# Routing logits of a mixture-of-experts block computed transposed, in four column strips of the TensorE array

## The chip, the cores and the metric

One NeuronCore of a Trainium2 chip. The metric is the device time of one execution in microseconds (us). Before the change the median of three runs is 702.88 us (702.61 to 703.27).

## What is computed

The input x is 8 sequences of 1024 tokens with 128 features, all in fp32. The kernel applies three layers, each with a residual: a feed-forward layer with half weight, a causal attention with one head, and the same feed-forward layer again.

```python
x = x + 0.5 * ffn(layernorm(x))
x = x + attention(layernorm(x))
x = x + 0.5 * ffn(layernorm(x))

# ffn(flat), T tokens, H = 128, E = 16 experts of width 64, and one shared expert of width 128
scores = sigmoid(flat @ Wg.T)                      # routing logits: T x 16
topk_idx, topk_w = route(scores, bias_corr)        # best 2 of 4 groups, then the best 4 experts
cw = zeros(T, E) with topk_w at topk_idx
hid = relu(einsum('th,eih->eti', flat, W1)) ** 2
out = einsum('eth,te->th', einsum('eti,ehi->eth', hid, W2), cw)
shared = relu(flat @ Ws1.T) ** 2 @ Ws2.T
```

The change touches the first of these products, the routing logits.

## The kernel before, in words

The 8192 tokens are 64 tiles of 128. Four tiles are a group of 512 tokens, so that a feed-forward phase has 16 groups. The 16 experts and the shared one are 1152 hidden rows, cut into nine chunks `c` of 128. For each chunk of a group TensorE makes the up product (`up`, lines 1237 to 1242), VectorE applies relu and the routing weights (`gate`, line 939), ScalarE squares twice, once rounded (lines 504 and 505), GpSimd takes the rounding remainder (line 379), and TensorE makes the down product (`down`, lines 1244 to 1254). Each of these products is split in three matmuls of rounded fp32 parts (`split3`, lines 1188 to 1190), each with a moving operand of 512 columns. The down product of chunk 5 is a plain fp32 matmul (line 1249), which the profile shows as two matmul instructions. The up product runs four chunks ahead of the down product (AHEAD = 4), over three PSUM banks.

Between these chunks, at fixed places of the unrolled loop over the nine chunks, each engine does the work of other groups. There is no scheduler: each engine has its own list of instructions, written out by hand, executes it in that order, and waits on semaphores. Bodies of two groups are repeated by a loop (`Fori`) on each engine. What is done for a group g + 4 or g + 3 while group g is computed:

- normalising: ScalarE and VectorE write `xn`, TensorE transposes it at c = 7 (`xn_transpose`, line 1219), ScalarE copies it out of PSUM into `x_f` at c = 8 (`x_copy`, line 472), rounds it later into `x_hi` at c = 6.
- logits (`logits`, line 1227), on TensorE at c = 2 for group g + 3: four fp32 matmuls, each with 128 tokens of `x_f` as stationary operand (128x128) and the 16 columns of `wgT` as the moving one. They give the tokens on the partitions and the experts on the columns. An fp32 matmul is two instructions with a weight load each, hence eight in a group.
- the sigmoid of the logits on ScalarE at c = 3 (line 486), and the routing on VectorE in ten parts from c = 3 on (`route`), which ends in `scw`.
- `w_transpose` on TensorE at c = 6 (line 1235), `wT_copy` on ScalarE at c = 7; SyncE stores `wT` to DRAM and loads it again, spread over the partitions, into `wb` (lines 305 and 318).
- the transpose of the last group's result on TensorE at c = 2 (`o_transpose`, line 1261), after ScalarE's `oT_copy` at c = 0, and the residual on VectorE (line 947).

In the feed-forward phases the logits of groups 0 to 2 are made before the loop. In the first phase this is in `opening` (TensorE lines 1264 to 1293, ScalarE lines 511 to 538), between the transposes of the weights (`weights_transpose`, line 1207). In the second it is inside the last steps of the attention: `start(k)`, called at the end of step k of the last two sequences. There the logits are made at k = 3, 5 and 11, and ScalarE's `sigmoid` stands at the same k.

The attention is computed per sequence: a score product with row maximum (line 1068), an exponential (line 611), transposes of the probabilities (line 1386), the product with the normalised tokens (line 1397) and one with `vw` (line 1410: fp32, 128x128 stationary and 128 moving columns, four matmuls of two instructions each).

Of the kernel before, what the change touches and what calls it, by code (L numbers as in the profile page):

```python
# [29 lines left out]
P = 128  # L30
# [12 lines left out]
class FfnSems:  # L43

    def __init__(self, sem, tag):
        self.stat = sem(tag + "stat")
        self.var_done = sem(tag + "var_done")
        self.rstd_done = sem(tag + "rstd_done")
        self.shift_done = sem(tag + "shift_done")
        self.xn_done = sem(tag + "xn_done")  # L50
        self.xn2_done = sem(tag + "xn2_done")
        self.xnT_done = sem(tag + "xnT_done")
        self.xf_done = sem(tag + "xf_done")
        self.xhi_done = sem(tag + "xhi_done")
        self.xlo_done = sem(tag + "xlo_done")
        self.lg_done = sem(tag + "lg_done")
        self.sig_done = sem(tag + "sig_done")
        self.denom_done = sem(tag + "denom_done")
        self.score_done = sem(tag + "score_done")
        self.route = sem(tag + "route")  # L60
        self.bias_done = sem(tag + "bias_done")
        self.wsum_done = sem(tag + "wsum_done")
        self.norm_done = sem(tag + "norm_done")
        self.scw_done = sem(tag + "scw_done")
        self.scwT_done = sem(tag + "scwT_done")
        self.wT_done = sem(tag + "wT_done")
        self.w_stored = sem(tag + "w_stored")
        self.w_loaded = [[sem(f"{tag}w_loaded{u}_{half}") for half in range(2)] for u in range(2)]
        self.up_done = sem(tag + "up_done")
        self.s_done = sem(tag + "s_done")  # L70
        self.sq_done = sem(tag + "sq_done")
        self.glo_done = sem(tag + "glo_done")
        self.down_done = sem(tag + "down_done")
        self.oT_copied = sem(tag + "oT_copied")
        self.oTr_done = sem(tag + "oTr_done")
        self.res_done = sem(tag + "res_done")
# [27 lines left out]
def macaron_kernel(nc, x, Qw, Kw, Vw, Wg, bias_corr, W1, W2, Ws1, Ws2, out):  # L104
    B, S, D = x.shape
    E, I, _ = W1.shape
    NT = B * S // P
    TG = 4
# [24 lines left out]
    with ExitStack() as ctx:  # L133
# [17 lines left out]
        w2_f = sb("w2_f", [P, len(WHOLE), D])  # L151
        wgT = sb("wgT", [P, E])
        qkT = sb("qkT", [P, 2, P])
# [73 lines left out]
        tr_ps = psum[:, 5, :]  # L227
        lg_ps = psum[:, 6, 0:P]
        wT_ps = psum[:, 6, P:2 * P]
        v_ps = psum[:, 7, :]  # L230
# [113 lines left out]
        def _(pool):  # L344
            nc.gpsimd.memset(ident[:], 0.0).then_inc(self_done, 1)
            nc.gpsimd.memset(maskb[:], 0.0).then_inc(self_done, 1)
            nc.gpsimd.memset(neg_half[:], -0.5).then_inc(const_done, 1)
            pool.wait_ge(self_done, 2)
            nc.gpsimd.affine_select(out=ident[:], in_=ident[:], compare_op=ALU.not_equal, fill=1.0, base=0,
# [95 lines left out]
        def _(sc):  # L445
# [21 lines left out]
            def ffn(F, phase):  # L467
                def x_copy(g, u, src):
                    sc.wait_ge(F.xnT_done, g + 1)
                    wait(sc, F.xlo_done, g - 1)  # L470
                    wait(sc, F.lg_done, g - 1)
                    copy(x_f[:, u, :], src).then_inc(F.xf_done, 1)

                def x_hi_copy(g, u):
# [4 lines left out]
                    copy(x_hi[:, u, :], x_f[:, u, :]).then_inc(F.xhi_done, 1)  # L479

                def sigmoid(g, u, src, by_exp=False):


                    sc.wait_ge(F.lg_done, g + 1)
                    wait(sc, F.wsum_done, g - 1)
                    nc.scalar.activation(scores[:, u].rearrange("p t e -> p (t e)"), src[:, 0:TG * E],
                                         ACT.Exp if by_exp else ACT.Sigmoid, scale=-1.0 if by_exp else 1.0).then_inc(F.sig_done, 1)
# [23 lines left out]
                def opening():  # L511

                    first_half(0)
                    sc.wait_ge(wgT_done, 1)
                    copy(wgT[:], lg_ps[:, 0:E]).then_inc(wgT_copied, 1)
                    x_copy(0, 0, tr_ps)
                    sigmoid(0, 0, lg_ps)
                    first_half(1)
                    x_hi_copy(0, 0)
                    weights_hi(0)  # L520
                    x_copy(1, 1, tr_ps)
                    weights_hi(1)
                    sigmoid(1, 1, lg_ps)
# [4 lines left out]
                    first_half(2)  # L528
                    x_copy(2, 0, tr_ps)
                    sigmoid(2, 0, lg_ps)  # L530
                    weights_hi(4)
                    first_half(3)
# [7 lines left out]
                def start(k):  # L540

                    for n in range(PREP):
                        if k == (1, 3, 9, 16)[n]:
                            first_half(n)
                        if k == (2, 4, 10, 17)[n]:
                            x_copy(n, n % UN, tr_ps)
                        if n < 3 and k == (3, 5, 11)[n]:
                            sigmoid(n, n % UN, tr_ps, by_exp=True)
                        if n < 2 and k == (8, 9)[n]:
# [7 lines left out]
                def body(i, first, last, extra):  # L557
                    for u in range(UN):
                        g = i * UN + u
                        for c in range(NCH):  # L560
                            j = u * NCH + c
                            if c == 0 and not (first and u == 0):
                                oT_copy(g - 1, 1 - u)
                            if c == 3 and not last:
                                sigmoid(g + 3, 1 - u, lg_ps)
# [617 lines left out]
        def _(pe):  # L1183
# [30 lines left out]
            def ffn(F, phase):  # L1214
# [7 lines left out]
                def logits(g, u, dst, wT_copied=0):  # L1222
# [3 lines left out]
                    for t in range(TG):  # L1226
                        ins = mm(dst[:, t * E:(t + 1) * E], x_f[:, u, t * P:(t + 1) * P], wgT[:], start=True, stop=True)  # L1227
                    ins.then_inc(F.lg_done, 1)

# [34 lines left out]
                def opening():  # L1264
# [4 lines left out]
                    xn_transpose(0, tr_ps)  # L1269
                    pe.wait_ge(wgT_copied, 1)  # L1270
                    logits(0, 0, lg_ps)
                    weights_transpose(0)
                    weights_transpose(1)
                    pe.wait_ge(F.xf_done, 1)
                    xn_transpose(1, tr_ps)
                    logits(1, 1, lg_ps)
                    weights_transpose(2)
                    weights_transpose(3)
                    w_transpose(0, wT_ps, sigmoids=2)
                    pe.wait_ge(F.xf_done, 2)  # L1280
                    xn_transpose(2, tr_ps)
                    logits(2, 0, lg_ps, wT_copied=1)
                    weights_transpose(4)
                    pe.wait_ge(F.xf_done, 3)
                    xn_transpose(3, tr_ps)
# [9 lines left out]
                def start(k):  # L1295


                    for n in range(PREP):
# [4 lines left out]
                        if n < 3 and k == (3, 5, 11)[n]:  # L1303
                            logits(n, n % UN, tr_ps)
                    if k == 12:
                        pe.wait_ge(F.sig_done, 3)
# [7 lines left out]
                def body(i, first, last, extra):  # L1314
                    for u in range(UN):
                        g = i * UN + u
                        for c in range(NCH):
                            j = u * NCH + c
# [3 lines left out]
                            elif not last:  # L1322
                                up(g + 1, (c + AHEAD) % NCH, m + AHEAD, (j + AHEAD) % (UN * NCH), 0)
                            if c == 2 and not last:
                                logits(g + 3, 1 - u, lg_ps, wT_copied=g + 2)
                            if c == 2 and not (first and u == 0):
                                o_transpose(g - 1, NG + 2 if last else g + PREP)
# [196 lines left out]
```

## Time and profile before

| | us |
|---|---|
| median of 3 runs | 702.88 |
| the profiled execution | 702.95 |
| span of its profile | 701.2 |
| outside the span | 1.75 |
| TensorE busy | 673.3 (96%) |
| VectorE busy | 567.5 (81%) |
| ScalarE busy | 529.6 (76%) |
| GpSimd busy | 438.2 (62%) |

The profile names the engines PE (TensorE's matmuls), PEld (its weight loads), DVE (VectorE), ACT (ScalarE), POOL (GpSimd) and SP (SyncE). Busy time is the union of an engine's instructions. Matmul records overlap each other, since the array is pipelined: what one costs is read from the distance between the starts of two successive ones. L1227 is line 1227 of the kernel.

### The profile page before, as it was taken

How to read it: one execution, taken by the hardware profiler on the slowest of the kernel's cores; microseconds unless marked ns; L12 is line 12 of the kernel's file. 1: busy time of each engine (PE TensorE's matmuls, PEld its weight loads, DVE VectorE, ACT ScalarE, POOL GpSimd, SP SyncE). 2: the span in 40 equal slices, each digit the busy share in tenths (PEclk: the TensorE clock that was granted, in tenths of full speed). 3: DMA queues.
4: the chain of work that ended last, by engine and by line, in shares of the span. 5: the costliest groups of instructions: out<-in, count | busy, mean ns of one | idle time of the engine just before them, and what ended most of it. 6: DMA issues, size and time to landing. Idle time of an engine off the chain costs nothing.

```text
span 701.2 us, 15091 instructions
## 1 busy us (share of the span) xinstructions
PE 673.3 (96%) x3367; PEld 527.5 (75%) x3367; DVE 567.5 (81%) x2586; ACT 529.6 (76%) x1094; POOL 438.2 (62%) x346
## 2 busy tenths in 40 slices
PE   4799999999999997999999999999999999999997
PEld 4567878888788875787778777778788887888775
DVE  5898998899888985666656678898988998889863
ACT  3578888888888866675566477659888788887875
POOL 3379888998889972000000021148889898898875
PEclk9999999999999999999999999999999999999999
DMA  9856776567765640000000000365776787767782
GB/s 246 196 124 138 162 165 145 124 147 154 162 143 123 152 90 0 1 1 1 0 1 0 0 0 1 71 134 115 158 166 140 166 179 171 165 139 174 166 178 72
DMA packets 53525, 78.37 MB, mean 112 GB/s; under 512 B 5216, under 2 KB 19184, under 8 KB 53488
## 3 DMA queue, kind: packets, MB, share of 16 engines
q1 hardware_dynamic: 51280, 77.36, 50.4%
q10 hardware_dynamic: 2208, 0.59, 0.4%
q8 instruction: 14, 0.23, 0.1%
q14 instruction: 23, 0.19, 0.1%
HBM read 72.70 MB, written 5.24 MB: 111 GB/s over the span
## 4 chain that ended last, share of the span: by engine, by line
PE 78%; DVE 10%; ACT 5%; issue 3%; POOL 1%; DMA 1%; POOLq 0%; DVEq 0%; ACTq 0%
PE psum L1188 18%; PE psum L1190 18%; PE psum L1189 18%; PE psum L1397 7%; PE psum L1227 4%; PE psum L1249 4%; DVE nmax L1068 3%; PE psum L1219 2%; PE psum L1261 2%; PE psum L1386 2%; ACT shared L611 2%; PE psum L1410 2%; DVE zn L1082 1%; DVE s_sb L939 1%; ACT wb L446 1%
## 5 line engine op out<-in xcount | busy, mean ns | idle before, releaser
L379 POOL TENSOR_TENSOR shared_r<-shared,shared_r 128x512 fp32r<-128x512 f32 x256 | 325.9, 1294 | 55.6 <-ACT shared L505 53.5
L939 DVE SCALAR_TENSOR_TENSOR s_sb<-psum,wb 128x512 f32<-128x512 f32 x256 | 175.5, 687 | 46.2 <-PE psum L1190 25.9
L505 ACT ACTIVATE shared<-s_sb 128x512 f32<-128x512 f32 x288 | 178.1, 620 | 28.6 <-DVE s_sb L939 28.6
L504 ACT ACTIVATE shared_r<-s_sb 128x512 fp32r<-128x512 f32 x256 | 159.8, 624 | 45.3 <-DVE s_sb L939 43.5
L1188 PE MATMUL psum<-x_hi,w_hi 128*128 128x512 f32 x288 | 127.2, 442 | 1.0 <-DVE x_sb L1094 0.5
L1190 PE MATMUL psum<-x_hi,w_lo 128*128 128x512 f32 x288 | 114.3, 397 | 0.0
L1189 PE MATMUL psum<-x_lo,w_hi 128*128 128x512 f32 x288 | 113.5, 394 | 0.0
L1188 PE MATMUL psum<-shared_r,w_hi 128*128 128x512 f32 x256 | 109.5, 428 | 0.8 <-POOL shared_r L379 0.7
L1189 PE MATMUL psum<-shared_r,w_hi 128*128 128x512 f32 x256 | 101.2, 395 | 0.0
L1190 PE MATMUL psum<-shared_r,w_lo 128*128 128x512 f32 x256 | 101.0, 395 | 0.0
L362 POOL TENSOR_TENSOR a_rstd<-a_mv,neg_half 128x8 f32<-128x8 f32 x8 | 13.1, 1636 | 116.4 <-DVE a_mv L758 116.4
L1188 PEld LDWEIGHTS psum<-x_hi,w_hi 128*128 128x128 f32 x288 | 54.5, 189 | 21.6 <-issue 7.2
L1189 PEld LDWEIGHTS psum<-x_lo,w_hi 128*128 128x128 f32 x288 | 54.4, 189 | 18.1 <-issue 7.2
L611 ACT ACTIVATE shared<-psum,nmax 128x128 f32<-128x128 f32 (+3 forms) x64 | 47.5, 742 | 23.5 <-DVE nmax L1068 22.2
L1190 PEld LDWEIGHTS psum<-x_hi,w_lo 128*128 128x128 f32 x288 | 54.2, 188 | 12.9
L1068 DVE TENSOR_REDUCE nmax<-psum 128x1 f32<-128x128 f32 (+3 forms) x64 | 47.5, 751 | 19.8 <-PE psum L1377 19.6
L1188 PEld LDWEIGHTS psum<-shared_r,w_hi 128*128 128x128 f32 x256 | 48.2, 188 | 13.6 <-POOL shared_r L379 3.8
L460 ACT ACTIVATE xn<-x_sb,shift,roots 128x128 f32 (+1 forms) x128 | 55.5, 481 | 2.7 <-DVE shift L778 2.7
L1190 PEld LDWEIGHTS psum<-shared_r,w_lo 128*128 128x128 f32 x256 | 48.1, 188 | 11.3
L1189 PEld LDWEIGHTS psum<-shared_r,w_hi 128*128 128x128 f32 x256 | 48.5, 189 | 7.7 <-issue 0.2
L398 POOL TENSOR_TENSOR roots<-powers,neg_half 128x8 f32<-128x8 f32 x28 | 45.8, 1637 | 9.2 <-DVE powers L919 5.5
L1397 PE MATMUL psum<-wb,zn 128*128 128x512 f32 (+3 forms) x128 | 47.2, 513 | 0.0
(166 smaller groups left out, 1301.5 us busy)
## 6 DMA issues: line engine op xcount, KB each, us to landing
wb<-scratch SPq DMA_DIRECT2D x128, 512.0 KB, 8.3
out<-x_sb SPq DMA_DIRECT2D x16, 256.0 KB, 9.8
x_sb<-in_L_attn_x SPq DMA_DIRECT2D x4, 256.0 KB, 6.1
scratch<-wT SPq DMA_DIRECT2D x32, 32.0 KB, 1.9
w_raw<-in_L_ffn_W ACTq DMA_DIRECT2D x1, 512.0 KB, 5.8
w_raw<-in_L_ffn_W SPq DMA_DIRECT2D x1, 512.0 KB, 6.7
w_raw<-in_L_ffn_Ws ACTq DMA_DIRECT2D x1, 64.0 KB, 8.6
w_raw<-in_L_ffn_Ws SPq DMA_DIRECT2D x1, 64.0 KB, 7.2
```

What stands on the lines that cost most here:

```text
L379: nc.gpsimd.tensor_tensor(g_lo[:, j % RING, :], g_f[:, j % RING, :], g_hi[:, j % RING, :].bitcast(F32), ALU.subtract).then_inc(F.glo_done, 1)
L398: nc.gpsimd.tensor_tensor(roots[:], powers[:], neg_half[:, 0:2 * TG], ALU.pow).then_inc(F.rstd_done, 1)
L460: ins = nc.scalar.activation(xn[:, t, :], x_sb[:, bass.ds(g * TG + t, 1), :].rearrange("p t d -> p (t d)"), ACT.Identity, bias=shift[:, t: ...
L504: nc.scalar.activation(g_hi[:, j % RING, :], s_sb[:, j % RING, :], ACT.Square)
L505: nc.scalar.activation(g_f[:, j % RING, :], s_sb[:, j % RING, :], ACT.Square).then_inc(F.sq_done, 1)
L611: nc.scalar.activation(prob[:, t % PR, 0:w], sc_ps[t % 2][:, 0:w], ACT.Exp, bias=nmax[:, u, t:t + 1], accum_out=rsum[:, u, t:t + 1]).then_ ...
L939: ins = nc.vector.scalar_tensor_tensor(s_, h_, 0.0, wb[:, u, c, :], ALU.max, ALU.mult)
L1068: nc.vector.tensor_reduce(nmax[:, u, t:t + 1], sc_ps[t % 2][:, 0:(t + 1) * P], AX.X, ALU.max, negate=True).then_inc(A.max_done, 1)
L1188: mm(out_, l_hi, r_hi, start=start, stop=False)
L1189: mm(out_, l_hi, r_lo, start=False, stop=False)
L1190: return mm(out_, l_lo, r_hi, start=False, stop=stop)
L1397: ins = mm(u_ps[:, q0:], zn[:, u, k, :], pT[half][:, k, q0:], start=(k == 0), stop=(k == last - 1))
```

## The change

The logits are computed the other way round. `wgT`, padded with zeros from 16 to 32 columns, is now the stationary operand (128x32), and the 128 tokens of a tile are the moving one (128 columns). The four tiles of a group write to partitions 0 to 31, 32 to 63, 64 to 95 and 96 to 127 of the same 128 PSUM columns, that is, each uses one strip of 32 columns of the array. ScalarE copies the 128x128 result to SBUF (`lgT_copy`), and one transpose on TensorE (`logits_transpose`) brings it back to tokens on the partitions. The sigmoid reads 16 of every 32 columns.

In the loop, TensorE makes the four matmuls at c = 0 where they were at c = 2, ScalarE copies at c = 1 ahead of its squares, and the transpose stands at c = 2. For the first group of the second phase (`held`) the places are c = 2, 2 and 3. In the opening the transposes stand one set of weight transposes later than the matmuls. In the last attention steps matmuls, copy and transpose stand at the same k.

```diff
+        EP = P // TG
+        wgT = sb("wgT", [P, EP])
+        lgT = sb("lgT", [P, P])
...
+            nc.gpsimd.memset(wgT[:, E:], 0.0).then_inc(wgT_copied, 1)
...
+                def lgT_copy(g, src):
+                    sc.wait_ge(F.lgT_done, g + 1)
+                    wait(sc, F.lg_done, g)
+                    copy(lgT[:], src[:, 0:P]).then_inc(F.lgT_copied, 1)
...
                     x_copy(2, 0, tr_ps)
+                    lgT_copy(2, lg_ps)
+                    weights_hi(4)
                     sigmoid(2, 0, lg_ps)
-                    weights_hi(4)
...
                         if n < 3 and k == (3, 5, 11)[n]:
+                            lgT_copy(n, tr_ps)
                             sigmoid(n, n % UN, tr_ps, by_exp=True)
...
+                            if c == (2 if held else 1) and not last:
+                                lgT_copy(g + 3, lg_ps)
                             if c == 3 and not last:
                                 sigmoid(g + 3, 1 - u, lg_ps)
...
                     for t in range(TG):
-                        ins = mm(dst[:, t * E:(t + 1) * E], x_f[:, u, t * P:(t + 1) * P], wgT[:], start=True, stop=True)
-                    ins.then_inc(F.lg_done, 1)
+                        ins = mm(dst[t * EP:(t + 1) * EP, 0:P], wgT[:], x_f[:, u, t * P:(t + 1) * P], start=True, stop=True)
+                    ins.then_inc(F.lgT_done, 1)
+
+                def logits_transpose(g, dst):
+                    pe.wait_ge(F.lgT_copied, g + 1)
+                    nc.tensor.transpose(dst[:, P:2 * P], lgT[:], ident[:]).then_inc(F.lg_done, 1)
...
                     logits(0, 0, lg_ps)
                     weights_transpose(0)
+                    logits_transpose(0, lg_ps)
...
                             logits(n, n % UN, tr_ps)
+                            logits_transpose(n, tr_ps)
...
-                            if c == 2 and not last:
+                            if c == (2 if held else 0) and not last:
                                 logits(g + 3, 1 - u, lg_ps, wT_copied=g + 2)
+                            if c == (3 if held else 2) and not last:
+                                logits_transpose(g + 3, lg_ps)
```

## Rows read from the trace of the kernel before

**Rows 1.** Busy time in one stretch of a group's length, all engines.

```profile
core 0: us, PE busy (x) PEld busy (x) DVE busy (x) ACT busy (x) POOL busy (x), PEclk, DMA share, GB/s
98.44:112.99 14.55, 14.55 (x73) 11.70 (x72) 13.28 (x65) 12.50 (x26) 12.96 (x11) 1.00 0.68 144
```

**Rows 2.** The chain that ended last, in order of time: start, us, what.

```profile
10.33 1.88 PE psum L1227 x8
...
24.11 1.89 PE psum L1227 x8
...
54.76 0.80 PE psum L1227 x8
...
229.42 0.80 PE psum L1227 x8
...
416.97 0.80 PE psum L1227 x8
...
471.98 0.80 PE psum L1227 x8
...
661.05 0.80 PE psum L1227 x8
```

**Rows 3.** In order of time, TensorE in one group: start, us, engine, line, operation.

```profile
98.27 0.96 PE L1227 MATMUL psum<-wgT,x_f 128*128 128x16 f32 x8
99.09 0.64 PE L1261 MATMUL psum<-ident,oT 128*128 128x128 f32 x4
99.48 0.48 PE L1188 MATMUL psum<-shared_r,w_hi 128*128 128x512 f32 x1
99.80 0.39 PE L1189 MATMUL psum<-shared_r,w_hi 128*128 128x512 f32 x1
```

**Rows 4.** In order of time, a single transpose on TensorE between two products.

```profile
105.29 0.27 PE L1235 MATMUL psum<-ident,scw 128*128 128x128 f32 x1
105.31 0.48 PE L1188 MATMUL psum<-shared_r,w_hi 128*128 128x512 f32 x1
105.63 0.40 PE L1189 MATMUL psum<-shared_r,w_hi 128*128 128x512 f32 x1
```

**Rows 5.** The chain that ended last, an fp32 product with 128 moving columns.

```profile
419.25 0.89 PE psum L1410 x8
```

**Rows 6.** In order of time, the turn from one group to the next, three engines.

```profile
93.84 0.40 PE L1190 MATMUL psum<-x_hi,w_lo 128*128 128x512 f32 x1
...
94.27 0.69 DVE L939 SCALAR_TENSOR_TENSOR s_sb<-psum,wb 128x512 f32<-128x512 f32 x1 [0.61 <-PE psum L1190]
...
97.76 0.62 ACT L505 ACTIVATE shared<-s_sb 128x512 f32<-128x512 f32 x1
99.32 0.63 ACT L505 ACTIVATE shared<-s_sb 128x512 f32<-128x512 f32 x1 [0.94 <-DVE s_sb L939]
100.83 0.63 ACT L504 ACTIVATE shared_r<-s_sb 128x512 fp32r<-128x512 f32 x1 [0.88 <-DVE s_sb L939]
...
109.53 0.60 ACT L446 ACTIVATE x_f<-psum 128x512 f32<-128x512 f32 x1
...
109.79 0.40 PE L1190 MATMUL psum<-x_hi,w_lo 128*128 128x512 f32 x1
110.03 0.40 PE L1188 MATMUL psum<-shared_r,w_hi 128*128 128x512 f32 x1
```

**Rows 7.** In order of time, opening: weight transposes, first sigmoid, a copy of 128x128.

```profile
12.03 1.95 PE L1207 MATMUL psum<-ident,w_raw 128*128 128x128 f32 x8
12.23 0.22 ACT L486 ACTIVATE scores<-psum 128x64 f32<-128x64 f32 x1 [2.04 <-PE psum L1227]
...
30.36 0.27 ACT L446 ACTIVATE m_f<-psum 128x128 f32<-128x128 f32 x1
```

**Rows 8.** In order of time, the attention step k = 3, ScalarE around the sigmoid.

```profile
417.01 0.60 ACT L446 ACTIVATE s_sb<-psum 128x512 f32<-128x512 f32 x1 [0.49 <-PE psum L1397]
...
417.81 0.22 ACT L486 ACTIVATE scores<-psum 128x64 f32<-128x64 f32 x1 [0.20 <-PE psum L1227]
```

More of the change, by code:

```diff
@@ L55, in __init__ @@
         self.xlo_done = sem(tag + "xlo_done")
+        self.lgT_done = sem(tag + "lgT_done")
+        self.lgT_copied = sem(tag + "lgT_copied")
         self.lg_done = sem(tag + "lg_done")
@@ L151, in macaron_kernel @@
         w2_f = sb("w2_f", [P, len(WHOLE), D])
-        wgT = sb("wgT", [P, E])
+        EP = P // TG
+        wgT = sb("wgT", [P, EP])
+        lgT = sb("lgT", [P, P])
         qkT = sb("qkT", [P, 2, P])
@@ L227, in macaron_kernel @@
         tr_ps = psum[:, 5, :]
-        lg_ps = psum[:, 6, 0:P]
-        wT_ps = psum[:, 6, P:2 * P]
+        lg_ps = psum[:, 6, 0:2 * P]
+        wT_ps = psum[:, 6, 2 * P:3 * P]
         v_ps = psum[:, 7, :]
@@ L470, in x_copy @@
                     wait(sc, F.xlo_done, g - 1)
-                    wait(sc, F.lg_done, g - 1)
+                    wait(sc, F.lgT_done, g - 1)
                     copy(x_f[:, u, :], src).then_inc(F.xf_done, 1)
@@ L485, in sigmoid @@
                     wait(sc, F.wsum_done, g - 1)
-                    nc.scalar.activation(scores[:, u].rearrange("p t e -> p (t e)"), src[:, 0:TG * E],
+                    nc.scalar.activation(scores[:, u], src[:, P:2 * P].rearrange("p (t e) -> p t e", t=TG)[:, :, 0:E],
                                          ACT.Exp if by_exp else ACT.Sigmoid, scale=-1.0 if by_exp else 1.0).then_inc(F.sig_done, 1)
@@ L514, in opening @@
                     sc.wait_ge(wgT_done, 1)
-                    copy(wgT[:], lg_ps[:, 0:E]).then_inc(wgT_copied, 1)
+                    copy(wgT[:, 0:E], lg_ps[:, 0:E]).then_inc(wgT_copied, 1)
                     x_copy(0, 0, tr_ps)
+                    lgT_copy(0, lg_ps)
                     sigmoid(0, 0, lg_ps)
@@ L521, in opening @@
                     x_copy(1, 1, tr_ps)
+                    lgT_copy(1, lg_ps)
                     weights_hi(1)
@@ L559, in body @@
                         g = i * UN + u
+                        held = phase == 1 and first and u == 0
                         for c in range(NCH):
@@ L1269, in opening @@
                     xn_transpose(0, tr_ps)
-                    pe.wait_ge(wgT_copied, 1)
+                    pe.wait_ge(wgT_copied, 2)
                     logits(0, 0, lg_ps)
                     weights_transpose(0)
+                    logits_transpose(0, lg_ps)
                     weights_transpose(1)
@@ L1277, in opening @@
                     weights_transpose(2)
+                    logits_transpose(1, lg_ps)
                     weights_transpose(3)
@@ L1283, in opening @@
                     weights_transpose(4)
+                    logits_transpose(2, lg_ps)
                     pe.wait_ge(F.xf_done, 3)
@@ L1316, in body @@
                         g = i * UN + u
+                        held = phase == 1 and first and u == 0
                         for c in range(NCH):
```

## The prediction

> **What bounds the kernel now.** I read the busy times by stretch first. Cut to the length of a group, they show TensorE busy for 14.55 of 14.55 us, VectorE for 13.28, GpSimd for 12.96, ScalarE for 12.50 [rows 1]. Then the chain that ended last. In both feed-forward phases it is TensorE alone, and the eight logit instructions stand in it 27 times: 13 times from 54.76 to 229.42, one every 14.555 us (174.66 over 12), and 14 times from 471.98 to 661.05 [rows 2]. They stand in it also in the opening, at 10.33 and 24.11, where eight take 1.88 us, and in the attention, at 416.97 (and at 443.12 in the same way, 0.80 us) [rows 2]. Last the order of time inside a group, for the distances between starts, because what comes off TensorE's list there comes off the end, as long as nothing else becomes late. A change of over 0.2%, 1.4 us, is what a measurement of this kernel can tell from none.
>
> **The change on TensorE, per group.**
> - Removed: from the first logit matmul at 98.27 to the next transpose at 99.09 are 0.82 us [rows 3], for eight instructions with 16 moving columns; their price is the 128-column weight load of each, about 0.10 us.
> - Added: one transpose. Alone it sits between 105.29 and the second product matmul at 105.63, 0.34 us, of which one matmul of 512 columns is 0.23 (109.79 to 110.03 is 0.24, less rounding) [rows 4, 6]. That leaves 0.11.
> - Added: the eight strip matmuls, L. The nearest row is an fp32 product with 128 moving columns, eight in 0.89 us, 0.111 each [rows 5]. No row shows a matmul on a part of the columns. The upper bound of overlap is two passes, 0.22 us, if all four strips run beside each other. With none it is 0.89. I take five passes, 0.555: the list is executed in order, the two instructions of a tile use the same strip, so the second waits for the first, and only the first of the next tile can run beside it. It lies halfway between the ends, so both stay in the range.
> - Unhindered, a group then takes 14.555 - 0.82 + 0.11 + 0.555 = 14.40 us, 0.155 less, over 27 groups 4.2 us.
>
> The Trainium skill (TensorE: Matmul & The Clock Gate, the part on packing small matmuls) says that matmuls on different column strips run at the same time, and gives 2.38 times the speed for three strips. By it L would be an estimate of 0.3 us or so, and the group 14.15; no row here shows it.
>
> **What becomes late.** The matmuls move from c = 2 to c = 0, and this puts them right behind the copy that feeds them. In the trace TensorE would come to them at 110.03, and ScalarE's copy to `x_f` runs from 109.53 to 110.13 [rows 6], 0.1 too late. A released matmul starts 0.05 later, and its weights can't be loaded ahead: 0.09, from 99.48 to 99.80, which is 0.32 instead of 0.23 [rows 3]. So even with nothing gained TensorE waits about 0.2 us here.
> Nor does the copy come earlier when TensorE gets faster, except in part. It ends a chain that begins with the last matmul of the up product of chunk 3 at 93.84: the gate at 94.27 waited 0.61 for it, VectorE works on from there, ScalarE waits 0.88 for VectorE at 100.83, and from there ScalarE has no idle time until the copy is done at 110.13 [rows 6]. That is 16.29 us, plus 0.14 for release and load, 16.43. TensorE's own distance from such a matmul to the place of the logits is 110.03 - 14.555 - 93.84 = 1.64. A wait at the logits delays the next up product of chunk 3, so two groups pass in one chain and one unhindered group without these 1.64: 2T = 16.43 + T0 - 1.64, T = (14.79 + T0)/2. With T0 = 14.40 this is 14.595, or 0.04 more than now. **The gain of 0.155 is eaten by the wait**, and the 27 groups lose 1.1 us.
>
> Covers that hold: `lgT_copy` (0.27, as the copy of 128x128 at 30.36 [rows 7]) follows the square that ends at 98.38, in ScalarE's idle time of 0.94 [rows 6]. It ends at 98.65, and TensorE wants it at 98.27 plus L plus the wait, 98.8 or later. Were that cover gone, it would cost up to 0.27 a group. The padded sigmoid reads as many elements as before. The products that now stand behind the logits have their squares and remainders long before. Nothing moves past a DMA queue: `wT_copy` and the loads behind it follow the same chain as `x_copy`.
>
> **Attention.** At k = 3, 5 and 11 TensorE waits inside the step: matmuls, then ScalarE's copy, then the transpose. At k = 3 ScalarE is busy with another copy until 417.61, and did the sigmoid at 417.81 [rows 8]. The new copy ends at 417.88, the transpose with its load is done for the queue at 418.13, and the product that began at about 417.77 begins 0.35 to 0.4 later. k = 3 and k = 11 are on the chain: +0.8 us; k = 5 is not (bounds 0 and 1.5 for all three).
>
> **Opening.** The first sigmoid began at 12.23 [rows 7]. The first logits now take 5 x 0.235 = 1.2 us instead of 1.88 [rows 2], but the transpose stands behind four weight transposes (half of 1.95 us [rows 7]): 10.33 + 1.2 + 0.98 + 0.24 and its way through the array, 12.9 or so, +0.7 on VectorE's routing, which bounds the next stretch. The logits at 24.11 return 0.7 [rows 2], and the new copy costs 0.27 in the first, ScalarE-bound part of the loop: +0.3 (bounds -0.4 and +1.3). The memset on GpSimd waits under the first loads: nothing, or with that cover gone under 0.3.
>
> **Sum.** +1.1 + 0.8 + 0.3 = +2.2 us on the profiled execution's 702.95, 705.1 us; the median of 702.88 is the same within 0.1.
>
> **The rivals.**
> - **Serial strips.** The change does not do what it says: the strips don't overlap, L = 0.89, T0 = 14.735, T = 14.76: +5.6 in the loops, +1.2 in the attention, +0.9 in the opening, 710.6. For it: the row of 0.89 is the only one like it. Against: different partitions of PSUM, different columns of the array. 0.17.
> - **The array runs empty at each change of shape.** A product matmul is 0.40 long and the next starts after 0.24 [rows 6]: 0.16 is the way through the array, hidden today. If it is exposed when full matmuls are followed by strips and again when strips are followed by full ones, L is 0.555 + 0.32 = 0.875, plus up to 0.1 for a load that can't go ahead: T = 14.755 to 14.82, +5.4 to +7.2, with some 1.5 elsewhere 710 to 711.7. It decides from L = 0.71 on, where T0 itself passes 14.555. No row shows a product with fewer than 128 stationary columns behind one with 128, so nothing speaks against it. The Trainium skill (TensorEngine Tiling, Key Properties) says that a change of tiling mode drains TensorE, which is this rival. 0.20.
> - **Full overlap.** L = 0.22, T0 = 14.07, T = 14.43: -3.4, with +0.7 and 0 elsewhere 700.2. This is the other side: faster. It decides below L = 0.47, where T falls under 14.555 in spite of the wait. 0.22.
> - **The wait gives way.** ScalarE's and VectorE's order moves with TensorE and the copy ends in time; L = 0.555: -4.2 + 1.1, 699.9. Against it: ScalarE's unbroken work before the copy. 0.07.
> - The forecast: 0.34, itself between 703.7 and 706.5.
>
> **How the numbers follow.** Faster: the third and fourth rival, less a little for partial overlaps that end within 0.2%: 0.27. Slower by over 0.2%: the first two and most of the forecast, 0.57. Within: 0.16. The range runs from 699.9 to 711; below lie parts of the two faster cases, above the dearest of the empty array.
>
> **What would show it.** Distances from the first strip matmul to the next product: 0.55 for the forecast, 0.2 or 0.9 for rivals. TensorE idle before L1227's weight loads, released by ScalarE's `x_f`, some 0.1 to 0.4 us each. The period of the groups 14.6. TensorE idle before the new transpose in the attention only. I am wrong in the main if the period is under 14.5 or over 14.7.

## The result and the profile after

Side by side on one chip, the changed kernel took 705.96 us (median of six runs, 705.6 to 707.39) and the kernel before 703.28 us (six runs, 702.61 to 705.07). The ratio is 1.0041, with an interval of [1.0027, 1.0054]: slower by 0.4%. The profiled execution took 705.92 us, 2.97 more than the one before.

The page of the changed kernel: span and busy times.

```profile
span 704.1 us, 15214 instructions
...
PE 666.1 (95%) x3401; PEld 503.0 (71%) x3401; DVE 568.9 (81%) x2586; ACT 535.9 (76%) x1128; POOL 438.8 (62%) x347
```

TensorE is busy for 7.2 us less than before (673.3), and yet the kernel is slower: TensorE now waits. The groups of instructions by line and form say for whom (busy us, mean ns of one, then the idle time just before them and what ended most of it):

```profile
L1244 PE MATMUL psum<-x_f,wgT 128*32 128x128 f32 x272 | 15.2, 296 | 6.4 <-ACT x_f L451 6.2
...
L1249 PE MATMUL psum<-ident,lgT 128*128 128x128 f32 x34 | 10.0, 295 | 5.2 <-ACT lgT L451 5.2
```

Both waits are for ScalarE: 6.2 us before the strips (L1244), for the copy of `x_f`; 5.2 us before the transpose (L1249), for the copy of the logits. The 5.2 are four waits, none in the steady loop: 2.66 in the first group of the first loop, and 0.50, 1.49 and 0.50 in the attention.

In order of time, the turn between two groups in the first loop, which answers to [rows 3, 6]:

```profile
110.22 0.60 ACT L451 ACTIVATE x_f<-psum 128x512 f32<-128x512 f32 x1
...
110.43 0.40 PE L1207 MATMUL psum<-x_hi,w_lo 128*128 128x512 f32 x1
...
110.87 0.16 PEld L1244 LDWEIGHTS psum<-x_f,wgT 128*32 128x32 f32 x8 [0.48 <-ACT x_f L451]
110.87 0.43 PE L1244 MATMUL psum<-x_f,wgT 128*32 128x128 f32 x8
...
111.22 0.50 PE L1205 MATMUL psum<-shared_r,w_hi 128*128 128x512 f32 x1
...
111.56 0.39 PE L1206 MATMUL psum<-shared_r,w_hi 128*128 128x512 f32 x1
```

The copy ends at 110.82 and the strips begin at 110.87, 0.44 behind the product before them, and 0.60 to 0.67 in every second group. In an unbroken stream two products are 0.235 apart. Of the difference 0.09 remains even without a wait (e10 below), so the wait for `x_f` is some 0.12 here and 0.3 in every second group. From the first strip matmul to the next product are 0.35 us (110.87 to 111.22), and that product is followed after 0.34 instead of 0.235.

**Where the 2.97 us are.** I followed one instruction that stands once in each group, the plain down product of chunk 5 (L1249 before, L1270 after). Its starts, before and after:

| stretch | before | after | difference |
|---|---|---|---|
| start to the second of the first loop | 60.07 | 60.81 | +0.74 |
| twelve periods of the first loop | 174.64 | 174.38 | -0.26 |
| rest of the first phase (to 262.94, 263.38) | 28.23 | 28.19 | -0.04 |
| attention (to 476.88, 478.96) | 213.94 | 215.58 | +1.64 |
| thirteen periods of the second loop | 189.48 | 190.43 | +0.95 |
| rest | 26.22 | 26.15 | -0.07 |

So four fifths of the loss (0.74 + 1.64 of 2.97) lie outside the steady loop, and the loops together lose 0.69. The table compares one execution of each kernel.

### The profile page after: what moved, and what is told of

The parts are those of the page before. It is cut to its first block, busy times and chain, and to the rows that moved or that the text cites. A ratio compares the mean times of both kernels' runs of the same rounds, so it can differ in the third digit from the quotient of the medians.

```text
span 704.1 us, 15214 instructions
## 1 busy us (share of the span) xinstructions
PE 666.1 (95%) x3401; PEld 503.0 (71%) x3401; DVE 568.9 (81%) x2586; ACT 535.9 (76%) x1128; POOL 438.8 (62%) x347
## 3 DMA queue, kind: packets, MB, share of 16 engines
HBM read 72.70 MB, written 5.24 MB: 111 GB/s over the span
## 4 chain that ended last, share of the span: by engine, by line
PE 62%; DVE 13%; ACT 11%; issue 9%; POOL 2%; DMA 2%; DVEq 1%; ACTq 0%; POOLq 0%; SPq 0%
PE psum L1205 14%; PE psum L1207 13%; PE psum L1206 13%; PE psum L1425 7%; ACT shared L515 3%; PE psum L1270 3%; PE psum L1414 2%; DVE s_sb L956 2%; DVE nmax L1085 2%; PE psum L1438 2%; PE psum L1236 2%; ACT shared_r L514 2%; ACT shared L628 2%; PE psum L1282 2%; DVE zn L1099 1%
## 5 line engine op out<-in xcount | busy, mean ns | idle before, releaser
L1205 PE MATMUL psum<-shared_r,w_hi 128*128 128x512 f32 x256 | 112.3, 439 | 0.9 <-POOL shared_r L384 0.9
L1206 PE MATMUL psum<-shared_r,w_hi 128*128 128x512 f32 x256 | 101.0, 394 | 0.0
```

The source lines that it names most:

```text
L1205: mm(out_, l_hi, r_hi, start=start, stop=False)
L1206: mm(out_, l_hi, r_lo, start=False, stop=False)
```

## The experiments

Ratios are to the kernel before, on the same chip. The changed kernel stands at 1.0041.

**e1: every group in the places of the first one of phase 2.** Strips at c = 2, copy at c = 2, transpose at c = 3.

```diff
-                        held = phase == 1 and first and u == 0
+                        held = True
```

> In the loop the strip matmuls stand at c = 2, ScalarE's copy at c = 2 and the transpose at c = 3 for every group, as the changed kernel has them for the first group of the second phase alone. Theory (the wait for x_f at c = 0 eats the gain): TensorE no longer waits there, a group costs what TensorE alone needs, 14.555 - 0.82 + 0.11 + 0.55 = 14.40 us against 14.54 in the changed kernel, 27 groups give back 3.8 us, about 702.2. Rival (the groups are bound by another chain, VectorE's or the loads of wb, and TensorE merely waits for that at the logits): the period stays at 14.54 and TensorE's idle time shows up elsewhere, 706.

Measured: 700.07 us, 0.9958 [0.9946, 0.9971]. The period is 14.326 us in nearly every group. In order of time, TensorE in one group of e1:

```profile
111.69 0.39 PE L1207 MATMUL psum<-x_hi,w_lo 128*128 128x512 f32 x1
112.01 0.43 PE L1244 MATMUL psum<-x_f,wgT 128*32 128x128 f32 x8
112.36 0.66 PE L1282 MATMUL psum<-ident,oT 128*128 128x128 f32 x4
112.78 0.48 PE L1205 MATMUL psum<-shared_r,w_hi 128*128 128x512 f32 x1
```

No wait stands before L1244. From product to strips are 0.32, or 0.09 more than the 0.235 of the stream, and the eight take 0.35 again. With the lateness of `x_f` gone the change does what it is for: 5.9 us less than the changed kernel. It even beat the theory, which had 14.40 for the group and 3.8 us in all. Between the two profiles, which are 6.17 us apart, the loops account for 5.24 (171.97 and 187.60 us for the two stretches of the table). Another 1.01 lies before the loop's second down product, which stands at 59.80 and not at 60.81: a gain from a shorter wait in the first group, which e4 and e8 below look at, and not from `x_f`.

**e10: only one chunk later.** Strips at c = 1, copy at c = 2, transpose at c = 3, in the loops.

```diff
-                            if c == (2 if held else 1) and not last:
+                            if c == 2 and not last:
                                 lgT_copy(g + 3, lg_ps)
...
-                            if c == (2 if held else 0) and not last:
+                            if c == (2 if held else 1) and not last:
                                 logits(g + 3, 1 - u, lg_ps, wT_copied=g + 2)
-                            if c == (3 if held else 2) and not last:
+                            if c == 3 and not last:
```

> In the loops the strips go one chunk later (c = 1), ScalarE's copy of the logits at c = 2, the transpose at c = 3; nothing else is changed. Theory (only the lateness of the copy of x_f, some tenths of a microsecond, costs anything): one chunk is enough, the wait of the strips for x_f is gone, the period of a group is 14.33 us and the time about 700. Rival (the strips need the place two chunks later, or holding the logits' copy back makes the transpose wait): period 14.5 or more, about 706.

Measured: 699.55 us, 0.9954 [0.9942, 0.9966]; the period is 14.355. In order of time:

```profile
109.85 0.60 ACT L451 ACTIVATE x_f<-psum 128x512 f32<-128x512 f32 x1
...
111.15 0.40 PE L1207 MATMUL psum<-x_hi,w_lo 128*128 128x512 f32 x1
111.47 0.43 PE L1244 MATMUL psum<-x_f,wgT 128*32 128x128 f32 x8
111.83 0.50 PE L1205 MATMUL psum<-shared_r,w_hi 128*128 128x512 f32 x1
112.17 0.40 PE L1206 MATMUL psum<-shared_r,w_hi 128*128 128x512 f32 x1
```

`x_f` is there at 110.45, 1.02 before the strips. Here they stand between two products, as in the changed kernel, and the three distances 0.32, 0.36 and 0.34 are the strips' price without any wait: 1.02 less two steps of 0.235, or 0.55. One chunk is enough.

What the 0.55 is made of, windows of 0.1 us and less show, which part the eight instructions. In order of time, and then the weight loads of the strips:

```profile
111.47 0.32 PE L1244 MATMUL psum<-x_f,wgT 128*32 128x128 f32 x4
...
111.61 0.29 PE L1244 MATMUL psum<-x_f,wgT 128*32 128x128 f32 x4
```

```profile
111.47 0.16 PEld L1244 LDWEIGHTS psum<-x_f,wgT 128*32 128x32 f32 x8 [0.36 <-issue]
```

Four of the eight start together (within 0.02 us), and the other four together, 0.13 later. Eight instructions on four strips are two passes: the overlap is full. The rest is the change of shape. In front it costs 0.09 (0.32 instead of 0.235): the first load starts only at 111.47, while the load of a product starts together with the product before it, 0.23 ahead. Behind, the next product starts 0.22 after the second four and is followed after 0.34, together 0.56 or a little less, where a pass of 0.11 and a step of 0.235 would be 0.35: some 0.2.

**e3: the copy of `x_f` earlier instead.** ScalarE does it at c = 7, the strips stay at c = 0.

```diff
-                            if c == 8 and not last:
+                            if c == 7 and not last:
                                 x_copy(g + PREP, u, tr_ps)
```

> The changed kernel with its strips at c = 0, but ScalarE copies x_f at c = 7, ahead of one pair of squares, instead of at c = 8. Theory (the end of this copy sets TensorE's wait): the copy ends about 1.05 us earlier, the wait goes, the period falls from 14.54 to 14.40 or less and the time to about 702.2. If another wait takes its place (the down product waiting for squares that are now later), the period stays above 14.5. Rival (another chain bounds): 706.

A miss, and the dearest one: 716.54 us, 1.0187 [1.0174, 1.02], the period 14.82 and 15.20 in turn. In order of time:

```profile
110.49 1.30 POOL L390 TENSOR_TENSOR x_lo<-x_f,x_hi 128x512 fp32r<-128x512 f32 x1
...
111.88 0.60 ACT L451 ACTIVATE x_f<-psum 128x512 f32<-128x512 f32 x1 [0.99 <-issue]
...
115.97 0.27 ACT L451 ACTIVATE lgT<-psum 128x128 f32<-128x128 f32 x1
...
116.29 0.33 PE L1249 MATMUL psum<-ident,lgT 128*128 128x128 f32 x1 [0.37 <-ACT lgT L451]
```

The copy comes no earlier, because it may not. ScalarE stands in front of it for 0.99. The transposes that it copies are long made (108.97 to 109.57), but the buffer of `x_f` that it writes is still read: GpSimd's `x_lo` of the group two before starts at 110.49, directly behind a remainder, and ends at 111.79, 0.09 before the copy. The code waits for it (`xlo_done`), and the distance is 0.08 to 0.09 in each of ten groups. The squares behind the copy, which the down products need, come that much later, and so does the copy of the logits. In the changed kernel, too, `x_lo` ends 0.08 before the copy starts (110.14 and 110.22), and in the kernel before (109.45 and 109.53). So two things hold the copy at almost the same moment, ScalarE's queue and GpSimd's. An earlier `x_lo` on GpSimd was not tried. Moving the consumer back, as in e10, needs neither.

**e6 and e7: what the strips are worth.** Both have e1's places. e6 sends all four tiles to the strip of partitions 0 to 31, so that none can overlap; its output lacks the logits of three tiles of four. e7 does without strips: `wgT` is padded to four 128x128 operands with the 16 columns in four places, and the four products are added up in PSUM.

```diff
-                        ins = mm(dst[t * EP:(t + 1) * EP, 0:P], wgT[:], x_f[:, u, t * P:(t + 1) * P], start=True, stop=True)
+                        ins = mm(dst[0:EP, 0:P], wgT[:], x_f[:, u, t * P:(t + 1) * P], start=True, stop=True)
```

```diff
+                        ins = mm(dst[:, 0:P], wgT[:, t, :], x_f[:, u, t * P:(t + 1) * P], start=(t == 0), stop=(t == TG - 1))
```

> As the first experiment, but all four tiles are written to the same strip (partitions 0 to 31), so that only the logits of the last tile of a group come out; ScalarE copies 32 partitions. Theory (the strips run beside each other, which is why eight matmuls take 0.35 us): on one strip they take eight times 0.11, 0.89 us, and a group 0.54 us more than with four strips, 27 groups 14 us: about 717. Rival (the short weight load is what makes them cheap, not the strips): no difference, 702.

> As the first experiment, but without strips: for each tile a weight of 128 columns, zero outside its 32, and the four products added up in the same PSUM tile. The result is the same, the whole array is used and nothing changes its shape. Theory (strips save, and the change of shape costs 0.10 to 0.11 each way): eight matmuls of 0.111, 0.89 instead of 0.55: 0.34 us more a group, 27 groups 9 us, about 711.5. Rival (the change of shape costs nothing, the 0.10 is the load that can't go ahead): 0.54 us more a group, 717.

Measured: e6 717.91 us, 1.0212 [1.0197, 1.0228], period 14.975; e7 711.07 us, 1.0115 [1.01, 1.0131], period 14.727. In order of time, e6 (the row at 116.40 is the last of the eight, from a window of its own) and then e7:

```profile
115.29 0.40 PE L1208 MATMUL psum<-x_hi,w_lo 128*128 128x512 f32 x1
115.61 1.06 PE L1245 MATMUL psum<-x_f,wgT 128*32 128x128 f32 x8
...
116.40 0.27 PE L1245 MATMUL psum<-x_f,wgT 128*32 128x128 f32 x1
116.61 0.66 PE L1283 MATMUL psum<-ident,oT 128*128 128x128 f32 x4
```

```profile
114.59 0.39 PE L1209 MATMUL psum<-x_hi,w_lo 128*128 128x512 f32 x1
114.59 1.09 PEld L1246 LDWEIGHTS psum<-x_f,wgT 128*128 128x128 f32 x8
114.82 1.05 PE L1246 MATMUL psum<-x_f,wgT 128*128 128x128 f32 x8
115.71 0.60 PE L1284 MATMUL psum<-ident,oT 128*128 128x128 f32 x4
```

From the first of the eight to the transposes behind them are 1.00 us on one strip, 0.89 on the whole array and 0.35 on four strips (e1). Inside, the distance from one to the next is the same on one strip (115.61 to 116.40, seven steps of 0.113) as on the whole array (eight of 0.111). The strips save passes: six of them, and e6's group is 0.65 longer than e1's. And the change of shape has a price of its own. Full products to strips are 0.32 in e1 and e6, full to full 0.23 in e7. In e7 the loads of the same place begin with the product before (114.59), in e10 only with the strips themselves. So the rival, "the load that can't go ahead", is no other cause: in these rows the load is held back where the shape changes, and not where it stays. Behind the strips the first transpose comes 0.21 after the last of the eight, and 0.11 in e7. In all, e1 has six passes less than e7 (0.65) and these prices more, and its group is 0.40 shorter, where my expectation had 0.34.

**e2 and e9: the attention.** e2 gives its three groups the old form (tokens stationary, sigmoid at once, no copy and transpose), e9 only the one at k = 5. The core of e2's edit:

```diff
                         if n < 3 and k == (3, 5, 11)[n]:
-                            logits(n, n % UN, tr_ps)
-                            logits_transpose(n, tr_ps)
+                            plain_logits(n, n % UN, tr_ps)
```

> The changed kernel, but the three logit computations inside the last attention steps (k = 3, 5, 11) in the old form: tokens stationary, no copy, no transpose. Theory (TensorE stands there while ScalarE finishes other work before the copy, 1.49 us at k = 5 alone): 1.8 us less, about 704.1, and the attention's last steps at the times of the kernel before. Rival (the stretch is set by other work that is merely shifted, such as the late start from the opening): under 0.5 us, 705.5 or more.

> The changed kernel with only the k = 5 group of attention in the old form; k = 3 and k = 11 keep the strips. Theory (k = 5 stands on the chain and costs 1.3 of attention's 1.8 us): about 704.7, with the row of attention's gap 1.2 us or more shorter than in the changed kernel. Rival (as the prediction had it: k = 3 and k = 11 cost 0.4 each and k = 5 nothing): 705.5 or more.

Measured: e2 704.25 us, 1.0021 [1.0012, 1.0031]; e9 704.81 us, 1.0027 [1.0016, 1.0039]. The stretch of the attention in the table is 213.89 in e2 and 214.18 in e9, against 215.58: of the 1.69 us that the three groups cost, k = 5 alone is 1.40 (one execution), and k = 3 and k = 11 together 0.3. The stretch is steady: 215.46 to 215.60 in all six profiles with four strips at the three places, 213.88 to 213.94 in all five with the old form, the kernel before among them. The edits that bring back the old form also let `x_copy` wait for `lg_done` in place of `lgT_done`; both are long reached where it stands. In order of time, the changed kernel at k = 3 and k = 5:

```profile
418.38 0.33 PE L1249 MATMUL psum<-ident,lgT 128*128 128x128 f32 x1 [0.50 <-ACT lgT L451]
...
423.40 0.43 PE L1244 MATMUL psum<-x_f,wgT 128*32 128x128 f32 x8
...
423.62 0.90 ACT L628 ACTIVATE shared<-psum,nmax 128x768 f32<-128x768 f32 x1
...
424.51 0.59 ACT L451 ACTIVATE z_hi<-psum 128x512 fp32r<-128x512 f32 x1
...
424.99 0.28 ACT L451 ACTIVATE lgT<-psum 128x128 f32<-128x128 f32 x1
...
425.32 0.33 PE L1249 MATMUL psum<-ident,lgT 128*128 128x128 f32 x1 [1.49 <-ACT lgT L451]
...
425.41 0.51 PE L1205 MATMUL psum<-z_hi,x_hi 128*128 128x512 f32 x1
```

ScalarE has an exponential and a copy ahead of the logits' copy at k = 5, and TensorE stands in front of the transpose for 1.49 us with the score product of the next step (425.41) queued behind it. In the kernel before only the sigmoid came that late (424.10), and TensorE did not wait for it: its logits began at 422.42 and the score product at 423.23. e9 in order of time shows this again, logits at 423.01 and the sigmoid only at 424.70:

```profile
423.01 0.96 PE L1266 MATMUL psum<-wgT,x_f 128*128 128x16 f32 x8
...
424.70 0.22 ACT L497 ACTIVATE scores<-psum 128x64 f32<-128x64 f32 x1
```

**e4: the opening in the old form.** The three groups there as before (`plain_logits` for `logits`, no `lgT_copy`, no transpose), the rest changed.

> The changed kernel, but the three logit computations of the opening in the old form. Theory: the first sigmoid comes 0.7 us earlier again, the third logits cost 0.7 more on TensorE; together the opening gives back 0.0 to 0.7 us of the 0.74 by which the changed kernel is behind when the loop starts, 705.3 to 706. If it gives back nothing, the 0.74 lies in the first body of the loop, in the copy that is new there.

Measured: 706.55 us, 1.0047 [1.0034, 1.006], no gain; the second down product stands at 61.17. Nothing in it says that the opening's own strips cost anything. What they had been suspected of lies behind them, in the first group of the loop. In order of time, the changed kernel there, and then its busy times in two stretches (length, PE, PEld, DVE, ACT, POOL, PEclk, DMA share, GB/s):

```profile
39.98 0.61 ACT L515 ACTIVATE shared<-s_sb 128x512 f32<-128x512 f32 x1
...
40.49 0.26 ACT L451 ACTIVATE lgT<-psum 128x128 f32<-128x128 f32 x1
...
40.80 0.47 PE L1249 MATMUL psum<-ident,lgT 128*128 128x128 f32 x1 [2.66 <-ACT lgT L451]
40.93 0.77 PE L1205 MATMUL psum<-shared_r,w_hi 128*128 128x512 f32 x1
```

```profile
40.00:42.00 2.00, 1.20 (x4) 1.00 (x5) 1.93 (x11) 1.38 (x4) 1.28 (x1) 0.56 1.03 220
42.00:44.00 2.00, 2.00 (x7) 1.56 (x6) 0.67 (x2) 1.26 (x3) 1.85 (x2) 0.58 1.06 203
```

The strips were done at about 34.5, but ScalarE's copy stands in its queue behind two squares, which wait for VectorE, the busiest engine of that stretch. TensorE waits 2.66 us, and on top of that its granted clock falls to the lower of its two levels (1.2 GHz): the six products from 40.93 to 43.64 take 2.71 us instead of 6 x 0.235 = 1.41, another 1.3 us. The kernel before had a clock of 1.00 there and no matmul of it waited longer than 0.33 between 34 and 48.

**e11: the old form in that one group.**

```diff
+                        old = phase == 0 and first and u == 0
...
-                                sigmoid(g + 3, 1 - u, lg_ps)
+                                (plain_sigmoid if old else sigmoid)(g + 3, 1 - u, lg_ps)
...
-                            if c == (2 if held else 0) and not last:
-                                logits(g + 3, 1 - u, lg_ps, wT_copied=g + 2)
+                            if c == (2 if held or old else 0) and not last:
+                                (plain_logits if old else logits)(g + 3, 1 - u, lg_ps, wT_copied=g + 2)
```

> The changed kernel with the old form in one group only, the first of the first loop; everything else keeps the strips. There TensorE stood 2.66 us at 40.80 for ScalarE's copy of the logits, whose place in ScalarE's queue is behind two activations that wait for VectorE, and ran its next six products at a granted clock of 0.56 to 0.58, 0.42 us each in place of 0.235. Theory (this wait and the clock after it are the 0.7 us by which the loop starts late): the second down product of the loop stands at 60.1 or before (60.81 in the changed kernel), no row of TensorE waits over 1 us between 36 and 46, the granted clock stays at 1.00 there, and the time is 704.5 to 705.3. Rival (VectorE's squares bound this stretch, the wait only stands in for another): the product stays at 60.7 to 60.9 and the time at 705.8 or more.

Measured: 705.34 us, 1.003 [1.0018, 1.0042]. The second down product, in order of time, and the busy times where the clock had been low:

```profile
59.30 1.02 PE L1296 MATMUL psum<-shared,w_f 128*128 128x512 f32 x2
```

```profile
40.00:42.00 2.00, 1.86 (x8) 1.12 (x7) 1.97 (x8) 0.72 (x2) 1.74 (x2) 1.00 1.03 224
42.00:44.00 2.00, 2.00 (x8) 1.28 (x8) 1.79 (x8) 1.95 (x5) 1.90 (x2) 1.00 1.05 206
```

The wait and the low clock are gone and the loop starts 1.51 us sooner (59.30, not 60.81), 0.77 sooner than before the change. The medians differ by 0.62 only, and their intervals overlap: that the mechanism is there is shown, that its whole price reaches the end is not. The profile is of the slowest of the six executions (706.75), and in it the second loop takes 192.60 us, 2.17 more than in the changed kernel. Single periods of 15.67, 15.60 and 15.31 stand in it; what made them long stays open.

**e5, e8 and e12: the parts together.** e5 is e1 with the old form in attention and opening; e8 is e1 with the old form in the attention; e12 is e8 with e11's edit.

> Strips in the loops alone, at c = 2 with the transpose at c = 3; opening and attention in the old form. If the parts add up, the time is the kernel before less 27 x 0.155 = 4.2 us: 699 us, faster than both. If the waits are not where the theory puts them, it stays at 702 or above.

> Strips held to one chunk later in every group (as in e1), the old form in the three groups of attention (as in e2), strips kept in the opening. Theory (the parts add: the loop gains from one place, attention loses from another): 700.1 of e1 less about 1.8 us, so 697.4 to 698.5, below e5 by about 1 us, and the down products of the loop stand at 45.5 and 59.8 as in e1. Rival (the opening and attention share one cover, or attention's gain was only there without the held strips): 699 or more.

> The kernel of e8 with the old form in the first group of the first loop as well. Theory (in e8's profile the clock fell to 0.50 behind a wait of 1.66 us and in e1's, of the same length, it did not, which is also why the times of e8 spread over 4.7 us): no wait there, no fall, the spread of the runs is under 2.5 us, and the median is 696 to 697.3. Rival (another stretch bounds the start of the loop and the spread is from elsewhere): 697.6 or more, spread as before.

Measured: e5 698.71 us, 0.9935 [0.9921, 0.9948]; e8 697.92 us, 0.9928 [0.9914, 0.9942]; e12 697.09 us, 0.9924 [0.9908, 0.9941]. All three beat both kernels, by 0.6 to 0.8% the one before; among themselves the intervals can't part them. The sum of the parts came out as expected for e5 (699) and e8 (697.4 to 698.5). e12's spread was 3.65 us (696.11 to 699.76), not under the 2.5 I expected, so this half of my theory fell, although the granted clock in its first group was 1.00. What its runs spread by stays open. A candidate, not tested, is VectorE's wait for the weights' DMA, which this view of e12's waits from 480 to 690 shows (us in total, times, longest). Against it: the kernel before has 8.8 us of it there, with the same longest wait of 2.8, and its twelve executions beside e12 lie within 1.09 us.

```profile
DVE s_sb L968 <- DMA wb<-scratch: 10.0, 9, 2.8
```

e8 and e1 show that the clock of the first group differs between executions. They wait 1.66 and 1.65 us for the copy, in the same steps of the kernel. The busy times behind it, e8 and then e1:

```profile
42.00:44.00 2.00, 1.91 (x7) 1.55 (x8) 1.80 (x7) 1.47 (x5) 1.85 (x2) 0.70 1.07 204
44.00:46.00 2.00, 2.00 (x6) 1.61 (x5) 1.61 (x10) 2.00 (x5) 2.00 (x2) 0.50 1.06 212
```

```profile
42.00:44.00 2.00, 1.48 (x7) 1.26 (x8) 1.92 (x7) 1.47 (x4) 1.89 (x2) 1.00 1.05 214
44.00:46.00 2.00, 2.00 (x11) 1.46 (x9) 1.85 (x12) 2.00 (x7) 1.90 (x3) 1.00 1.07 217
```

In e8 the clock fell and the second down product stands at 60.89, in e1 it did not and it stands at 59.80, 1.09 sooner. Other profiles do either, too: behind a wait of 1.65 it fell in e10 (0.52 from 42 to 44) and in e5, behind 1.66 it held in e7 (1.00), and behind 2.59 to 2.66 it fell in all five that have such a wait. So e5's late start (61.16) is no proof against the old form in the opening. The profiles of e5 and e8 are of their slowest executions (701.07 and 700.63), so they say little of the medians.

## Why the prediction was right, and which of its steps were not

The number held (705.1 forecast, 705.96 measured; +2.2 against +2.97 us in the profiled executions, +2.7 between the medians), and so did its main step, that the wait for `x_f` eats the gain. But the strips' term came out by luck, two errors that cancel, and so in part did the sum: 1.1 for the loops, 0.8 for attention and 0.3 for the opening were 0.69, 1.64 and 0.74. The range, 699.9 to 711, was wide.

- **The strips, L = 0.555.** Right in size: 0.55 by e10's distances; e10's period of 14.355 gives 0.51. The reasoning behind it was wrong, and its hitting is luck. It said that only the first instruction of the next tile runs beside the second of the last, hence five passes of 0.111. There are two, with all four strips at work, about 0.25 us. And it put nothing for the change of shape, which costs 0.09 before and some 0.2 behind. Two rivals had one half each: full overlap the passes (0.22), the empty array the change of shape (0.32 for both). Their sum, 0.54, is close to the measured price.
- **Unhindered group, 14.40.** 14.355 in e10, 14.326 in e1.
- **The wait for `x_f`.** Right. The step from 14.40 to 14.595 was 0.195. Over both loops the period is (174.38 + 190.43)/25 = 14.592, against (172.32 + 187.45)/25 = 14.391 in e10, uneven groups in both: 0.20. e10 and e1 show that the wait is what eats the gain. What holds the copy was seen in part only: beside ScalarE's queue it is GpSimd's `x_lo` (e3), which the prediction does not name. But the kernel before has a mean of (174.64 + 189.48)/25 = 14.565 over the same groups, since its second loop is uneven too, so the loops lost 0.69 us, not 1.1. In the first loop the period came out at 14.53, in the second at 14.65. There the changed kernel's waits were longer. These two lines are from its view of waits, 480 to 690:

```profile
DVE s_sb L956 <- DMA wb<-scratch: 9.2, 12, 1.9
...
PEld psum L1244 <- ACT x_f L451: 4.0, 7, 0.9
```

  The kernel before has 8.8 us of the first and nothing of the second: TensorE had slack where the strips now have none. That the DMA's delay is what reaches TensorE there is my reading; no run took it away.
- **`lgT_copy` is covered.** Right in the steady loop (no wait of L1249 there), wrong in its first group, where the prediction gave "0.27 in the first, ScalarE-bound part of the loop" and the wait was 2.66 us and a lower clock.
- **Attention, +0.8, "k = 5 is not" on the chain.** This step failed: +1.64, above even the bound of 1.5, and of the three places' 1.69 the one at k = 5 has 1.40 (e9). The sigmoid at k = 5 was off the chain because TensorE did not wait for it. The transpose made TensorE wait for ScalarE's place in its queue, behind the exponential. k = 3 and k = 11 together cost 0.3, not 0.8.
- **Opening, +0.3.** The +0.74 at the second down product is two terms. e11 shows the opening itself 0.77 *sooner* than before (one execution each). The first sigmoid came at 12.00, not at "12.9 or so", as this row of the changed kernel, in order of time, shows:

```profile
12.00 0.22 ACT L496 ACTIVATE scores<-psum 128x64 f32<-128x64 f32 x1 [0.96 <-PE psum L1249]
```

  The strips there took 0.59 us (10.04 to the weight transposes at 10.63), where the prediction had five passes of 0.235, 1.2 us. The first group of the loop then lost 1.51, which no step of the prediction had.
- **The rivals.** Serial strips fell with e6 and e7. Full overlap was right about the overlap and wrong in L, as it had no price for the change of shape; its way of being faster (a group under 14.555) is what e1 and e10 reach by another road. The empty array was right about that price and wrong in its base of five passes. "The wait gives way" did not happen by itself; made to happen, in e10, it gave 699.55 us where that rival said 699.9.
- **The pages.** The Trainium skill (TensorE: Matmul & The Clock Gate, Part 3) gives 2.38 times for three strips. The trace has 1.00 us on one strip against 0.35 on four, 2.9 times with the way to the next instruction counted in, and the passes alone overlap in full; that page was nearer than my five passes. The Trainium skill (TensorEngine Tiling, Key Properties) says that a change of tiling mode drains TensorE; the distances agree, with 0.09 us before the strips and some 0.2 behind.

## What to carry to other kernels

An operation that is split in two, with another engine's copy between the halves, needs two places: put the second half where that engine's *queue*, not only the engine, has reached the copy. Look at each place in which the operation stands, the first pass of a loop and the one-off stages too, since the cover differs: here four such places cost some 3 us (1.51 and 1.69, by e11 and e2) and the steady groups 0.7. When a consumer waits some tenths of a microsecond for a copy in every round, move the consumer one step later before touching the producer's order, and before moving the producer look at who still reads the buffer that it writes. A term that comes out right is not yet understood: the strips' 0.55 was two errors, and only the single instructions told.

## What was new about the hardware

- Eight instructions of 128 moving columns and 32 stationary ones (four fp32 matmuls) on four strips are two passes: four start within 0.02 us, the others 0.13 later. On one strip they follow each other at 0.113, on the whole array at 0.111: a quarter of the columns is no faster, only the running side by side is.
- Strips begin 0.09 us late behind a product, and their weights are not loaded ahead. The product that follows them loses some 0.2. Eight full-width instructions in the same place (e7) lose nothing in front, and their loads begin 0.23 ahead.
- TensorE's clock fell behind a wait of 1.66 us in e8 and held behind one of 1.65 in e1, in the same steps. In e8 it fell only after work had begun again: the wait ended at 42.09, the matmul at 42.49 still took 0.39, the one at 43.08 took 0.63. Such a wait costs its own length in some executions and 1.1 us more in others (1.3 in the changed kernel, behind 2.66). The Trainium skill (TensorE: Matmul & The Clock Gate, Part 1) says of the clock's rise at the start of steady work that its moment varies from run to run. For the fall these two traces show the like.
